# Second attention: where the row sums are inverted, and who multiplies them by the coefficients

## The reference, cut to what matters

```python
scores = jnp.einsum('bhqd,bhkd->bhqk', q, k) / math.sqrt(HD)
scores = jnp.where(causal, scores, -jnp.inf)
aw = jax.nn.softmax(scores, axis=-1)
...
lam = lam1 - lam2 + LAMBDA_INIT
aw = aw.reshape(Bx, NQ, 2, Sx, Sx)
aw = aw[:, :, 0] - lam * aw[:, :, 1]
attn = jnp.einsum('bhqk,bhkd->bhqd', aw, v) * (1.0 - LAMBDA_INIT)
```

## Time and profile before

| what | value |
| --- | --- |
| median of three runs | 614.96 us (609.89 to 614.98) |
| the profiled execution's own time | 612.89 us |
| its span, first to last instruction | 611.1 us |
| mean granted TensorE clock | 0.907 of full speed |
| PE busy | 510.2 us (83%) |
| DVE busy | 425.6 us (70%) |
| ACT busy | 335.5 us (55%) |
| POOL busy | 311.1 us (51%) |

### The profile page before, as it was taken

The page is one execution under the profiler, slowest core; times in us unless marked ns, Lnnn a source line. Parts: engine busy times, 40 slices in busy tenths (PEclk is TensorE's granted clock), DMA queues, the critical chain, the costliest instruction groups (busy, mean ns, idle before and its releaser), DMA issues. The chain is left out here.

```text
span 611.1 us, 12837 instructions
## 1 busy us (share of the span) xinstructions
PE 510.2 (83%) x3886; PEld 358.0 (59%) x3886; DVE 425.6 (70%) x1656; ACT 335.5 (55%) x559; POOL 311.1 (51%) x472
## 2 busy tenths in 40 slices
PE   4978559967688999999999999998463699999970
PEld 2657459953355444444544544444362599999970
DVE  4785646646679899999999999945528445454536
ACT  4745336623654677777777777786241354545423
POOL 3541055327553685665685667555200477777630
PEclk9998669988699899999999999999855599999995
DMA  9400112322653545566435444231371111111205
GB/s 324 191 2 18 51 40 70 68 74 63 139 101 91 113 94 127 129 139 136 123 107 130 100 117 96 76 65 38 142 244 45 31 44 50 48 49 49 49 30 204
DMA packets 90496, 58.20 MB, mean 95 GB/s; under 512 B 72673, under 2 KB 76770, under 8 KB 88614
## 3 DMA queue, kind: packets, MB, share of 16 engines
q1 hardware_dynamic: 81550, 41.18, 26.7%
q0 software_dynamic: 3744, 7.68, 4.9%
q10 hardware_dynamic: 5136, 8.52, 4.0%
HBM read 37.72 MB, written 19.63 MB: 94 GB/s over the span
## 5 line engine op out<-in xcount | busy, mean ns | idle before, releaser
L1703 DVE CUSTOM_DVE_ANT_1 banks<-banks,a_mask 128x480 f32<-128x480 f32 (+14 forms) x480 | 190.0, 459 | 14.9 <-PE banks L1960 13.2
L1839 ACT ACTIVATE a_prob_<-banks 128x1024 f32<-128x1024 f32 x160 | 154.9, 1022 | 47.9 <-PE banks L1974 47.9
L1541 POOL TENSOR_SCALAR_AFFINE_SELECT a_prob_<-a_prob_ 128x512 f32<-128x512 f32 x128 | 80.8, 635 | 74.6 <-ACT a_prob_ L1839 73.6
L1960 PE MATMUL banks<-a_k_u_,a_q_u_ 72*128 72x512 bf16 (+15 forms) x512 | 103.0, 291 | 4.3 <-DVE a_neg_max_ L1703 4.1
L1960 PEld LDWEIGHTS banks<-a_k_u_,a_q_u_ 72*128 72x128 bf16 x512 | 64.7, 148 | 67.1 <-DVE a_neg_max_ L1703 34.8
L1191 PE MATMUL banks<-f_hgt,f_w_now 128*112 128x128 f32 (+1 forms) x808 | 102.9, 280 | 0.0
L952 POOL DMA_INDIRECT f_hg<-scratch_h_rows,r_source x62 | 59.8, 964 | 77.0 <-DVE r_source L292 47.8
L1974 PE MATMUL banks<-a_q_u_,a_k_x_ 75*128 75x512 bf16 x320 | 97.9, 387 | 0.7 <-ACT a_prob_ L1839 0.7
L1191 PEld LDWEIGHTS banks<-f_hgt,f_w_now 128*112 128x112 f32 (+1 forms) x808 | 97.6, 187 | 0.0
L1986 PE MATMUL banks<-a_prob_,a_v_g_ 128*32 128x512 f32 (+3 forms) x1024 | 83.7, 444 | 0.4 <-POOL a_prob_ L1541 0.4
L1703 DVE DVE_READ_ACCUMULATOR2_ANT a_neg_max_<- 128x1 f32 x512 | 72.1, 143 | 0.0
(11 more groups left out here) (240 smaller groups left out, 676.9 us busy)
## 6 DMA issues: line engine op xcount, KB each, us to landing
a_q_u_<-scratch_q_parts SPq DMA_DIRECT2D x15, 576.0 KB
scratch_o_rows<-a_o_sb_ ACTq DMA_DIRECT2D x28, 256.0 KB, 2.3
w<-in_w SPq DMA_DIRECT2D x2, 2048.0 KB, 10.3
w<-in_w SPq DMA_DIRECT2D x2, 1792.0 KB, 9.9
scratch_q_parts<-a_part_ SPq DMA_DIRECT2D x24, 128.0 KB
a_k_u_<-scratch_k_parts SPq DMA_DIRECT2D x48, 48.0 KB
scratch_h_rows<-r_h SPq DMA_DIRECT2D x8, 256.0 KB, 2.0
f_back<-scratch_back_rows SPq DMA_DIRECT2D x4, 512.0 KB, 5.1
```

The source lines that it names most:

```text
L1541: nc.gpsimd.affine_select(out=block_p, in_=block_p, pattern=[[0, JH], [1, P]], compare_op=ALU.is_ge, fill=0.0, base=0, channel_multiplier= ...
L1703: last = nc.vector.tensor_tensor_reduce(out=found, in0=found, in1=mask[:, :, TG - 4 * (t + 1):], scale=-1.0, scalar=-MASKED, op0=ALU.add, ...
L1839: nc.scalar.activation(prob[g % 2][:, 2 * e:2 * e + 2].rearrange("p s j t c -> p (s j) t c"), PS[:, b0:b0 + 2, :].rearrange("p s (j c t) - ...
L1960: last = nc.tensor.matmul(PS[:, a % 3, off:off + width], queries[:, g % 2, :, t], k_u[r][:, :, g % 2 * TG:g % 2 * TG + 4 * (t + 1)], start ...
```

## The change

For batches 0 to 2, DVE's `factors` is called two maxima tiles later in the same step of the loop, behind `maximum(g+3, 1)`. It now makes the reciprocal alone and signals a new semaphore `inverted`. GpSimd waits for that in `signed(b)`, behind the last `causal` of the same group, and multiplies `r_b` by `coef_p` in place, which sets `r_ready`. For the last batch DVE still does both. SP, PE and ACT have the same instructions as before in the same order.

```diff
+            def signed(b):
+
+                gp.wait_ge(inverted, b + 1)
+                nc.gpsimd.tensor_scalar(r_b[:], r_b[:], coef_p[:], None, ALU.mult).then_inc(r_ready, 1)
...
+                if g >= KVH and g % KVH == NORM_AT:
+                    signed(g // KVH - 1)
                 if g >= KVH:
                     b, n = g // KVH - 1, g % KVH - NORM_AT - 3
...
-                ch.link(nc.vector.reciprocal(r_b[:, 0:count], l_b[b % 2][:, 0:count]))
-                nc.vector.tensor_scalar(r_b[:, 0:count], r_b[:, 0:count], coef_p[:], None, ALU.mult).then_inc(r_ready, 1)
+                inverse = nc.vector.reciprocal(r_b[:, 0:count], l_b[b % 2][:, 0:count])
+                if b < B - 1:
+                    inverse.then_inc(inverted, 1)
+                else:
+                    ch.link(inverse)
+                    nc.vector.tensor_scalar(r_b[:, 0:count], r_b[:, 0:count], coef_p[:], None, ALU.mult).then_inc(r_ready, 1)
...
             for g in range(GROUPS):
-                if g >= KVH and g % KVH == NORM_AT:
-                    factors(g // KVH - 1)
                 for ahead in range(2 if g == 0 else LEAD, LEAD + 1):
                     for a in range(NA):
                         if g + ahead < GROUPS:
                             maximum(g + ahead, a)
+                        if a == 1 and g >= KVH and g % KVH == NORM_AT:
+                            factors(g // KVH - 1)
```

More of the change, by code:

```diff
@@ L1334, in phase_attention1 @@
         o_out = [semaphore(f"o_out{r}_") for r in range(2)]
+        inverted = semaphore("inverted")
         r_ready, r_out, r_in, n_mul, at_ready = (semaphore(n) for n in ("r_ready", "r_out", "r_in", "n_mul", "at_ready"))
```

## The result

The changed kernel takes 610.95 us (median of 22 runs, 608.43 to 611.89), against 613.38 us for the kernel before (22 runs, 609.89 to 615.57). The ratio is 0.9959, with a 95% interval of 0.9945 to 0.9973, so 2.5 us less (1.7 to 3.4). The profiled execution has a span of 609.1 us, against 611.1 before. Forecast were 2.6 us and 611.4 us.

What follows compares the result with a forecast made beforehand. PE was taken to set the pace in the second attention's loop, DVE close behind. Per call 1.05 - 0.19 = 0.86 us, three calls 2.6 us, giving 611.4 us as the middle of 610.3 and 612.4; range 606.8 to 614.4 us.

Steps and rivals of the forecast that it cites:

- The sum: Whole kernel: 0.86 us gained per call, three calls, 2.6 us in all, giving 611.4 us.
- The 1.05 us that the reciprocal's new place frees: Groups with factors: with the reciprocal behind tile 1, PE's waits before tiles 3 and 4 go, 1.05 us per call.
- The loss at tile 5, 0.19 us: Groups with factors: tile 2 starts 0.37 us late on DVE, so PE's tile 5 comes 0.19 us late.
- the 7.2 to 7.3 named as the sign: PE's x24 rows of groups 11, 19 and 27 should come 7.2 to 7.3 us apart instead of 8.11.
- the 0.92 us from the start of tile 2 to PE's tile 5: Spacing from DVE's tile 2 to PE's tile 5 in the old group with factors, used to place tile 5 at 269.59.
- The removed 0.80 us of the multiplication: DVE, three times: without the multiplication, 1.78 us of work ahead of tile 0 becomes about 0.87 us.
- The reciprocal doesn't wait for GpSimd: DVE's reciprocal at its new place is not held by GpSimd's port use, so its 0.87 us stand.
- The rival of 1.1 us: Reciprocal waits for GpSimd's instruction at its new place, starting 0.49 us later: gain only 1.1 us, 612.9 us; chance 0.05.
- The multiplication on GpSimd: GpSimd, three times: 0.46 us, bounds nothing and 1.10 us, costed at nothing because waits behind it cover it.
- The slower rival: GpSimd's multiplication outruns 2.4 us of waits, delaying the causal block of 287.89; at 5 us, 619 us; chance 0.03.
- The new waits: `signed` waits for `inverted`, set about 269.6; `r_ready` comes some 6 us later, about 281.9, with some 3 us cover left.
- The clock: PE's clock rise at another point of the experts shifts time 2 us either way, 609 to 614 us; chance 0.09.

Runs made afterwards that it cites:

- reciprocal twice: Changed kernel with a second reciprocal into an unused buffer ahead of its own, behind tile 1: groups with factors 7.94 us, median 611.21 us, ratio 0.9993.
- The multiplication moved alone: Changed kernel with the reciprocal back in front of tile 0, multiplication still on GpSimd: groups with factors 7.21 us, median 610.86 us, ratio 0.9977.

## Why the prediction was right, and where not

- **The sum** (2.6 us forecast, 3.0 in the groups, 2.5 by the ratio): right in sign and size. That 2.5 stands closer to it than 3.0 does is luck, since the interval of 1.7 to 3.4 us holds both. So is part of the nearness of 611.4 to 610.95 us: it was the middle between two bases, and the 22 runs put the kernel before at 613.38, near that middle.
- **The 1.05 us that the reciprocal's new place frees**: the 1.05 us and the waits were read rightly, but their end was put down to the new place alone. The lateness at tile 2, 1.2 us in the earlier trace rows too, would have cost 0.88 of the 1.05 by itself (reciprocal twice). The multiplication moved alone brings 0.91 of the 1.00. The prediction never asked what each edit does without the other. Done alone, they bring 2.7 and 1.9 us, and together 3.0.
- **The loss at tile 5, 0.19 us**: 0.06 measured, 0.05 to 0.07 by the groups, so these came out at 7.11 to 7.13 us and not at the 7.2 to 7.3 named as the sign. The mis-sized term is the 0.92 us from the start of tile 2 to PE's tile 5, taken from the earlier trace rows. In that group PE was still at scores 3 until 277.50, so the spacing held PE's work as well as DVE's. In the changed kernel it is 276.68 to 277.40, 0.72 us. The error made the forecast 0.4 us too cautious.
- **The removed 0.80 us of the multiplication**: right as a duration. But the multiplication takes 0.29 us, a third of its 0.88, once GpSimd's long instruction is out of its way. The end of L1717 just behind the end of L1519 was seen and used for the reciprocal only, not for the question of how this instruction could be made short where it stood.
- **The reciprocal doesn't wait for GpSimd**: right. It starts at 275.82 and takes 0.94 us, while GpSimd's 1.12 us instruction, begun at 275.19, is running until 276.31. The rival of 1.1 us falls.
- **The multiplication on GpSimd**: 0.61 us for 0.46 forecast, inside its bounds, and free for PE, as the kernel without a reciprocal shows.
- **The slower rival**: right in kind, wrong in its place. It said that the last causal block decides, from 2.4 us on. It is the first, from 0.6 + 2.2 = 2.8 us on. The text gave that block 3.5 us. By its own row it had 2.5 in the kernel before: PE's x8 row follows the row of 277.50 at 277.81, and a group of 7.05 us later is 284.86. In the changed kernel it has 2.2.
- **The new waits**: `r_ready` came as late as said, about 282.0, and the transfer left at 285.47, up to 0.3 us later behind its group than before. The text set `inverted` at about 269.6 on the plain clock, but its own figures give 267.80 + 0.95 = 268.75. Nothing hung on that.
- **The clock**: right that it can move the time by 1 to 2 us. In the profiled executions it did so at two places, 1.2 us each and in opposite directions, of which only the one in the experts was named. PE was taken to be at half clock right behind the loop, where the kernel before still has 1.00 in 426 to 428 us.

## What to carry to other kernels

When two edits attack one stall, work out each without the other. Here the later wait of the chain was nearly as long as the one in sight, and so the edit that shortened the work did nearly all. A spacing between two engines' rows prices a wait only if the waiting engine had nothing else to do in between. And before a slow small instruction is moved to another engine, look at what the other engines run at that moment. An end that falls just behind another engine's end is a sign of waiting, and that engine's order can be the cheaper thing to change. Swapping it is also the test.

## What the runs showed of the hardware that was not expected

- DVE's multiplication of 128x128 f32 by a per-partition scalar takes 0.88 us beside a 1.1 us GpSimd instruction, and 0.29 to 0.30 us beside ones of 0.2 us.
- GpSimd takes 0.61 us for the same operation, more than the 0.456 us of its two-input product of the same size.
- Two DVE products of 64x512 with both inputs in SBUF take 2.55 and 3.01 us in two executions beside GpSimd's product and sum, and 1.29 us alone.
